# A transformer tower on one core: four max products moved into the expert stage, side stages moved to other tiles, a memset moved to another engine, and two sets of transfers queued elsewhere

## The chip, the cores and the metric

The kernel runs on one core of one Trainium2 chip. The metric is the device time of one execution in microseconds, as a median of repeated runs. Five engines work side by side: TensorE (products), VectorE, ScalarE, GpSimd, and SyncE, which here only issues the transfers.

## The reference

`x` is (16, 64, 128, 64). For each of the 16 items the tower computes, with 1024 tokens of width 64:

```
h = tokens(x)                                    # patches of 16, rfft, @ W.T
h = h + attn0(layernorm(h))                      # 8 heads of 8, bias from a table
h = h + routed_ffn(layernorm(h))                 # in, two layers (one of 16 experts by item part + shared), out
h = h + attn1(layernorm(h))                      # 8 heads of 8
h = h + moe(layernorm(h))                        # gate, top 2 of 8 experts, exact gelu
```

with softmax attention in both layers: `softmax(q @ k.T * scale + bias) @ v`, then a projection.

## The kernel before

**Tiles.** The attentions of all items are one stream of 4096 tiles, 128 for each of the 32 attentions, in `SUPERS` = 4 supertiles of `SUPER` = 32. For a tile `n` TensorE does three things. `scores` (L897): 128 keys by 512 queries in bf16 parts, including three rows with the negated maxima of the queries, written to one of three PSUM banks, the ring `RING`; ScalarE empties it with the exponential (L1101). `nat` (L885), here called the max product: the same kind of product, queries by keys, for a later tile; VectorE reduces it to a row maximum (L1294, `reduce_tile`). It runs `SUPER + LEAD` = 46 tiles ahead of `scores`, over three banks `NAT` of its own. `pv` (L911), the value product: once in four tiles, four heads together, when n % 4 is 1. Each engine's program goes over the tiles in order, and each engine does its instructions in order.

**The maxima's way.** When the last max product of a supertile is reduced, `super_max` (VectorE) and `split_max` (GpSimd, four small steps) make three bf16 parts. The side stage `TN` (`turn`, tiles 23, 55, 87, ...) transposes them on TensorE (L869), VectorE copies them out (L1287), and SyncE writes them into the query rows with four transfers (`max_dma`, L607). `scores` of the next supertile, nine tiles after `TN`, waits for these.

**Pairs and side stages.** `program_phases` makes a serial start, a `first` phase of 128 tiles, 15 pairs of 256 tiles, a `last` phase of 128, and a serial end. Pair `r` runs attention 0 of item r+1 and attention 1 of item r. All other work is cut into named side stages that `side_schedule` puts on tiles of the pair. For each tile TensorE does the side stages first, then its score and max product; ScalarE does the exponential first and then the side stages; VectorE the reduction and then the side stages; GpSimd and SyncE follow the tile order too. The names:

- `LX`: load of an item's x rows, in two halves of 1 MB (L532, two transfers of 512 KB each, SyncE). `TOKA`, `TOKB`, `TOKC`: tokens from the first half, the second half (L750, 8 f32 products), and their transposition (L757).
- `LN1`, `LN2`: layernorm by VectorE and GpSimd in turn; `TR`: transposition of its result (L765). `QK`, `QV`: projections (L772, L727); ScalarE empties QK's two banks, VectorE those of QV. GpSimd then splits q and k into parts (L1400 to L1406), `SCR` writes them to DRAM scratch (L625, L627), and `RL`, the reload, fetches them in 24 transfers into the rows that the products read (L641, L645), 12 for heads 0 to 3 and 12 for heads 4 to 7. `VC` copies v.
- `CT` (two parts), `OTR`, `PROJ`: end of an attention. `H1`, `L0`, `L1`, `WO`: routed feed-forward; `WCL`, `WCA`: loading and summing its weights.
- `GATE`, `RANK`, `MT`, `FW`, `FY0` to `FY8`, `OUT`: mixture of experts. `FW`, the expert stage (L840, L842), runs its eight experts in all four banks, two for each expert in turn: expert e waits for the Gelu of expert e - 2 (L1073). No tile is in work meanwhile.
- `ZK` (pairs 0 and 14): zeroes rows of a key buffer that changes its use.

`SIDE_BANKS` says which stages write into the second side bank. That bank is one of the three ring banks; `score_ring` keeps it from the tiles for `SIDE_TILES` = 4 tiles, so the tiles have two banks in that time.

`middle_of` is the chain from the end of attention 0 to the q, k, v of attention 1, laid out wide over the second half of a pair. `short_middle_of` is the same chain where it has to be done within one half: at the start of pair 0 and in the second half of pair 14.

**SyncE.** `SCR` and `RL` in most phases wait for the score product of their own tile before each transfer is issued. In pairs 0 and 14 they did not: all 24 transfers of the reload stand on one tile (`every=0`) and are issued as soon as the scratch is written. The x rows' second half stands on tile 83 and the max rows on tile 87, both issued in that order.

Of the kernel before, what the change touches and what calls it, by code (L numbers as in the profile page):

```python
# [54 lines left out]
TURN = 23  # L55
SIDE_TILES = 4
# [70 lines left out]
def side_schedule(r, f1, f2, f3, first=False, last=False):  # L127
# [9 lines left out]
    def middle_of(b, n):  # L137

        for dn, name, *more in ((0, "CT"), (5, "OTR"), (8, "PROJ", 0), (13, "LN1", "a"),
# [3 lines left out]
            put(n + dn, name, b, *more)  # L143

    def short_middle_of(b, n):

        for dn, name, *more in ((0, "CT"), (4, "OTR"), (6, "PROJ", 0), (8, "LN1", "a"),
# [4 lines left out]
            put(n + dn, name, b, *more, every=0 if name in ("SCR", "RL") else 2)  # L152
# [25 lines left out]
    if f2:  # L178
        put(78, "TOKA", r + 2)
        put(83, "LX", r + 2, 1)  # L180
        put(97, "TOKB", r + 2)
        put(102, "TOKC", r + 2)
        put(105, "LN1", r + 2, "0")
# [8 lines left out]
    if f3:  # L192
        put(96, "WCL", r + 1)
        put(121, "WCA", r + 1)
        if last:
            put(130, "ZK", 0)
            short_middle_of(r + 1, 135)
        else:
            middle_of(r + 1, 133)
# [123 lines left out]
def super_of(kind, it, q):  # L323
# [12 lines left out]
    return a, b, q % 2, q % SUPERS // 2  # L336

# [10 lines left out]
def tower_kernel(nc, x, w_dft, dft, const, onehot, qk_w, v_w, pw, qk_scale, wi, routed, shared, wo, bo,  # L348
                 table, route, wg, w1, b2, w2, out):
    with ExitStack() as ctx:  # L350
# [165 lines left out]
        def _(eng):  # L516
# [144 lines left out]
            def body(kind, it, n0, side, found):  # L661
# [7 lines left out]
                for n in sorted(side):  # L669
                    for k, stage in enumerate(side[n]):  # L670
                        if stage[0] == "TN":
                            max_dma(kind, it, stage[1], found[n, k])
                        else:
                            side_stage(stage, found[n, k],
                                       n0 + n if kind == "first" or kind == "pair" and 0 < it < B - 2 else 0)
# [6 lines left out]
        def _(eng):  # L682
# [55 lines left out]
            def side_stage(stage, n, tile, slot):  # L738
# [89 lines left out]
                elif name == "FW":  # L828
# [4 lines left out]
                    for e in range(E):  # L833
# [9 lines left out]
                        mm.then_inc(fw_ready, 1)  # L843
                    eng.wait_ge(he_ready, at(E * b + E - 1))
# [72 lines left out]
            def body(kind, it, n0, side, found):  # L917
# [11 lines left out]
                for n in range(n_tiles(kind)):  # L929
                    if kind == "first" and n == LATE:  # L930
                        eng.wait_ge(s_rest, N_SET[s_rest])
                    for k, stage in enumerate(side[n]):
                        if stage[0] == "TN":
                            turn(n0, stage[1], found[n, k])
                        else:
                            side_stage(stage, found[n, k], n0 + n, n)
                    ahead = n + SUPER + LEAD
                    q = ahead // SUPER
# [4 lines left out]
                    if kind != "last" or q < SUPERS:  # L943
                        nat(kind, it, n0, ahead)
# [172 lines left out]
        def _(eng):  # L1117
# [63 lines left out]
            def side_stage(stage, n):  # L1181
                name, b, k, is_last, *more = stage
                if name == "ZK":
                    eng.wait_ge(st_ready, ATTN if b == 1 else ATTN * (2 * B - 2))
                    eng.memset(KA[b][64:K_MAX, :, :], 0.0).then_inc(keys_clear, 1)
                elif name == "TOKC":
# [117 lines left out]
            def body(kind, it, n0, side, found):  # L1304
# [11 lines left out]
                for n in range(n_tiles(kind)):  # L1316
# [5 lines left out]
                    ahead = n + SUPER + LEAD  # L1322
                    q = ahead // SUPER
                    if kind != "last" or q < SUPERS:
                        reduce_tile(n0, ahead)
                        if ahead % SUPER == SUPER - 1:
                            super_max(n0, q)
# [10 lines left out]
        def _(eng):  # L1338
# [31 lines left out]
            def side_stage(stage, n):  # L1370
# [3 lines left out]
                if name == "LN1":  # L1374
# [88 lines left out]
            def body(kind, it, n0, side, found):  # L1463
# [6 lines left out]
                for n in range(n_tiles(kind)):  # L1470
                    if kind == "first" and n == LATE:
                        eng.wait_ge(s_rest, N_SET[s_rest])
                    ahead = n + SUPER + LEAD
                    q = ahead // SUPER
                    if ahead % SUPER == SUPER - 1 and (kind != "last" or q < SUPERS):
                        split_max(n0, q)
# [77 lines left out]
```

## Time and profile before

| | |
|---|---|
| median of 3 runs | 4034.71 us (4033.22 to 4037.4) |
| profiled execution | 4041.78 us, span 4040.0 us |
| TensorE busy | 3811.9 us (94%) |
| VectorE busy | 2886.2 us (71%) |
| ScalarE busy | 2619.9 us (65%) |
| GpSimd busy | 860.0 us (21%) |
| mean granted TensorE clock | 0.98 |

The span is the profiled time between the first and the last instruction. Busy shares are means over all stages. In the timelines, a product's row gives its modelled duration of 0.38 us, while the next may start 0.22 us later; the pace is read from the starts. What stands in brackets is the engine's idle time before the instruction and what ended it.

### The profile page before, as it was taken

What the parts mean: (1) busy time and instruction counts of PE and PEld (TensorE: products, weight loads), DVE (VectorE), ACT (ScalarE), POOL (GpSimd) and SP (SyncE); (2) the same over time, 40 slices, a digit from 0 to 9 for tenths busy, and PEclk for the clock granted to TensorE, in tenths of its full rate; (3) what the DMA queues carried; (4) which work ended last, traced back from release to release, by engine and by line L of the source; (5) the groups of instructions that cost most, each with busy time, mean ns of one, the idle gap of its engine ahead of it and who ended that gap; (6) DMA issues with size and microseconds to landing.
All of it is one profiled execution on the core that took longest, in us unless ns stands there. A gap on an engine that the chain in (4) does not pass through costs nothing.

```text
span 4040.0 us, 62363 instructions
## 1 busy us (share of the span) xinstructions
PE 3811.9 (94%) x21508; PEld 1330.2 (33%) x21508; DVE 2886.2 (71%) x4955; ACT 2619.9 (65%) x4768; POOL 860.0 (21%) x1263
## 2 busy tenths in 40 slices
PE   6988999999999999999999999999999999999896
PEld 3223333333333333333333333333333333333232
DVE  3866767778686777867678676777867677777672
ACT  0555767667676666767667676666767667676564
POOL 4122113122121322213122121312213122121211
PEclk7899999999999999999999999999999999999998
DMA  5203211222012122111222122122111222111100
GB/s 106 40 15 60 43 36 33 46 48 44 22 35 56 33 43 43 37 34 33 46 48 43 27 38 49 32 43 47 38 29 33 50 44 43 31 36 25 28 6 6
DMA packets 119067, 156.36 MB, mean 39 GB/s; under 512 B 24847, under 2 KB 66575, under 8 KB 118717
## 3 DMA queue, kind: packets, MB, share of 16 engines
q1 hardware_dynamic: 118753, 152.38, 19.0%
q8 instruction: 172, 2.82, 0.3%
q14 instruction: 142, 1.16, 0.1%
HBM read 120.01 MB, written 29.36 MB: 37 GB/s over the span
## 4 chain that ended last, share of the span: by engine, by line
PE 81%; ACT 8%; issue 4%; DVE 3%; SPq 2%; DMA 1%; POOL 1%; ACTq 0%; POOLq 0%; DVEq 0%
PE acc L911 23%; PE side_st L897 21%; PE nat L885 19%; PE side_st L854 3%; PE side_st L750 3%; PE side_st L727 2%; ACT prob L1101 2%; PE side_st L840 2%; ACT hidden L1073 2%; PE side_st L807 1%; DVE tile_max L1294 1%; ACT hidden L1019 1%; PE side_st L772 1%; SPq L525 1%; PE side_st L765 1%
## 5 line engine op out<-in xcount | busy, mean ns | idle before, releaser
L1294 DVE TENSOR_REDUCE tile_max<-nat 128x1 f32<-128x512 f32 x4096 | 2585.7, 684 | 1002.6 <-PE nat L885 972.0
L1101 ACT ACTIVATE prob<-side_st 128x512 f32<-128x512 f32 x4096 | 2205.8, 600 | 1271.7 <-PE side_st L897 1236.8
L897 PE MATMUL side_st<-q_rows,k_rows 99*128 99x512 bf16 x4096 | 1562.6, 384 | 45.9 <-ACT prob L1101 28.9
L885 PE MATMUL nat<-k_rows,q_rows 96*128 96x512 bf16 x4096 | 1532.2, 385 | 30.2 <-DVE tile_max L1294 24.0
L911 PE MATMUL acc<-prob,v_padded 128*32 128x512 f32 x8192 | 1096.1, 607 | 14.5 <-ACT prob L1101 13.5
L897 PEld LDWEIGHTS side_st<-q_rows,k_rows 99*128 99x128 bf16 x4096 | 398.6, 98 | 1213.9 <-ACT prob L1101 812.1
L885 PEld LDWEIGHTS nat<-k_rows,q_rows 96*128 96x128 bf16 x4096 | 400.8, 98 | 508.4 <-DVE tile_max L1294 276.1
L1455 POOL TENSOR_SCALAR max_parts<-neg_max 128x16 bf16<-128x16 f32 x128 | 26.5, 207 | 1868.4 <-DVE neg_max L1301 1868.3
L911 PEld LDWEIGHTS acc<-prob,v_padded 128*32 128x32 f32 x8192 | 162.3, 108 | 377.4 <-ACT prob L1101 216.0
L840 PE MATMUL side_st<-ln_rows,w 64*128 64x512 f32 x512 | 139.5, 622 | 28.7 <-ACT hidden L1073 23.2
L1380 POOL TENSOR_SCALAR ln_s<-ln_s 128x8 f32<-128x8 f32 x64 | 13.0, 203 | 676.8 <-DVE ln_s L1202 673.2
L1073 ACT ACTIVATE hidden<-side_st,b 128x1024 f32<-128x1024 f32 x128 | 139.0, 1113 | 18.7 <-PE side_st L842 18.5
L750 PE MATMUL side_st<-x_rows,w_patch 128*128 128x512 f32 x248 | 121.4, 635 | 10.2 <-DMA x_rows<-in_x 10.2
L854 PE MATMUL side_st<-hidden,w 128*64 128x512 f32 x512 | 113.4, 595 | 0.0
L1392 POOL TENSOR_TENSOR ln_s<-ln_s,const 128x8 f32<-128x8 f32 x64 | 105.6, 1650 | 12.1 <-POOL ln_s L1389 12.1
L840 PEld LDWEIGHTS side_st<-ln_rows,w 64*128 64x128 f32 x512 | 41.5, 187 | 101.8 <-ACT hidden L1073 81.5
L750 PEld LDWEIGHTS side_st<-x_rows,w_patch 128*128 128x128 f32 x248 | 50.7, 206 | 66.1 <-issue 51.0
L1406 POOL TENSOR_TENSOR hidden<-hidden 128x1024 bf16<-128x1024 f32 x32 | 68.3, 2133 | 5.9 <-POOL hidden L1404 5.9
L1402 POOL TENSOR_TENSOR hidden<-hidden 128x1024 f32<-128x1024 f32 x32 | 68.2, 2131 | 6.2 <-POOL hidden L1400 6.2
L1394 POOL TENSOR_TENSOR centred<-centred,ln_s 128x512 f32<-128x512 f32 x64 | 66.8, 1043 | 11.4 <-POOL ln_s L1392 11.4
L1385 POOL TENSOR_TENSOR squares<-centred 128x512 f32<-128x512 f32 x64 | 66.6, 1041 | 11.7 <-POOL centred L1383 11.7
L807 PE MATMUL side_st<-hidden,group_weights 128*128 128x256 f32 x256 | 66.0, 379 | 1.4 <-ACTq L1038 1.3
(124 smaller groups left out, 1994.5 us busy)
## 6 DMA issues: line engine op xcount, KB each, us to landing
q_rows<-q_scratch SPq DMA_DIRECT2D x576, 64.0 KB
k_rows<-k_scratch SPq DMA_DIRECT2D x192, 192.0 KB
x_rows<-in_x SPq DMA_DIRECT2D x62, 512.0 KB, 6.3
q_scratch<-hidden SPq DMA_DIRECT2D x32, 384.0 KB
k_scratch<-hidden SPq DMA_DIRECT2D x96, 128.0 KB
group_weights<-in_routed SPq DMA_DIRECT2D x64, 129.0 KB, 2.1
q_rows<-max_rows SPq DMA_DIRECT2D x512, 3.0 KB
out_h<-out_rows SPq DMA_DIRECT2D x16, 256.0 KB, 2.1
```

Source lines behind the costliest of these rows:

```text
L727: mm = eng.matmul(both[par][:, j * cols:j * cols + cols], rows[half, j * P:j * P + P], w[half, :], start=(j == 0), stop=True, skip_group_c ...
L750: mm = eng.matmul(bk[:, :], Wf[:, j, :, :].rearrange("p a o -> p (a o)"), xv[:, :, j, :], start=(j == 0), stop=(j == 3))
L807: mm = eng.matmul(bk[:, c:c + 256], WC[:, g, ll, 0:HID], HE[:, ll, g * 256:g * 256 + 256], start=(g % 2 == 0), stop=True, skip_group_check ...
L840: eng.matmul(both[par][:, :], W1[half, e, :], XT[half, :], start=True, stop=False)
L854: mm = eng.matmul(SIDE[0][half, :], w, m, start=(e < 0), stop=(e == E - 1), skip_group_check=True)
L885: eng.matmul(NAT[use % len(NAT)][:, :], QA[u][0:K_NAT, h, c:c + P], KA[u][0:K_NAT, h, kh * 512:kh * 512 + 512], start=True, stop=True)\
L897: eng.matmul(RING[TILE_BANK[n0 + n]][:, :], KA[u][0:K_ALL, h, t * P:t * P + P], QA[u][0:K_ALL, h, half * 512:half * 512 + 512], start=True ...
L911: mm = eng.matmul(ACC[32 * hh:32 * hh + 32, :], VZ[buffer_of(a, b)][:, t, HEADS * g + hh, :], prob[:, (first_tile + hh) % TILES, :], start ...
L1073: eng.activation(HE[:, e, :], both[:, :], ACT.Gelu, bias=b1[:, e:e + 1]).then_inc(he_ready, 1)
L1101: eng.activation(prob[:, n % TILES, :], RING[TILE_BANK[n0 + n]][:, :], ACT.Exp).then_inc(exp_done, 1)
L1294: eng.tensor_reduce(mx[:, q % 2, j // 8, j % 8 // 2, j % 2:j % 2 + 1], NAT[use % len(NAT)][:, :], AX.X, ALU.max).then_inc(nat_free, 1)
L1392: eng.tensor_tensor(ln_s[:, 4, :], ln_s[:, 3, :], half_pow, ALU.pow).then_inc(ln_p, 1)
```

## The change

- `max_tiles` is new and replaces the fixed `n + SUPER + LEAD` on TensorE, VectorE and GpSimd. On the tile with `FW` the max products run `AHEAD` = 4 tiles further ahead: four of them stand between the products of the second and the third expert. Every third tile after it then has none, until the lead is 46 tiles again (tiles 53, 56, 59 and 62 of the pair).
- Side stages in `middle_of` (which starts at tile 135 and not 133), `short_middle_of` and the token stages of the next item but one stand on other tiles.
- The x rows' second half stands on tile 88, behind the max rows of tile 87; `TOKB` on 99 (97 before), `TOKC` on 103 (102).
- In pairs 0 and 14 the reload's transfers stand on a tile each, and those of its second half 15 tiles further on; and these pairs too wait for the score product of each tile.
- `ZK` goes from VectorE to GpSimd, with the waits that it needs there.

```diff
+AHEAD = 4
 def middle_of(b, n):
-        for dn, name, *more in ((0, "CT"), (5, "OTR"), (8, "PROJ", 0), (13, "LN1", "a"),
-                                (20, "LN2", "a"), (21, "BO"), (29, "TR", "a"), (33, "H1"), (38, "L0"),
-                                (44, "L1"), (49, "WO"), (56, "LN1", "1"), (62, "LN2", "1"),
-                                (71, "TR", "1"), (77, "QK", 1), (80, "QV", 1)):
+                                (20, "LN2", "a"), (21, "BO"), (29, "TR", "a"), (32, "H1"), (37, "L0"),
+                                (43, "L1"), (49, "WO"), (56, "LN1", "1"), (62, "LN2", "1"),
+                                (71, "TR", "1"), (76, "QK", 1), (85, "QV", 1)):
 def short_middle_of(b, n):
-                                (42, "TR", "1"), (44, "QK", 1), (46, "QV", 1), (54, "SCR", 1),
-                                (54, "VC", 1), (58, "RL", 1)):
-            put(n + dn, name, b, *more, every=0 if name in ("SCR", "RL") else 2)
+                                (43, "TR", "1"), (46, "QK", 1), (49, "QV", 1), (55, "SCR", 1),
+                                (55, "VC", 1)):
+            put(n + dn, name, b, *more, every=0 if name == "SCR" else 2)
+        for k, part in enumerate(side_parts([("RL", b, 1)])):
+            at[n + (58 + k if k < 4 * PARTS else 73 + k)].append(part)
 # side_schedule
-        put(83, "LX", r + 2, 1)
-        put(97, "TOKB", r + 2)
-        put(102, "TOKC", r + 2)
-        put(105, "LN1", r + 2, "0")
+        put(88, "LX", r + 2, 1)
+        put(99, "TOKB", r + 2)
+        put(103, "TOKC", r + 2)
+        put(106, "LN1", r + 2, "0")
-            short_middle_of(r + 1, 135)
+            short_middle_of(r + 1, 132)
-            middle_of(r + 1, 133)
+            middle_of(r + 1, 135)
+def max_tiles(side, n):
+    def extra(m):
+        for slot in range(m, max(m - 3 * AHEAD, -1), -1):
+            if any(x[0] == "FW" for x in side.get(slot, ())):
+                return AHEAD - (m - slot) // 3
+        return 0
+    return range(n + SUPER + LEAD + (extra(n - 1) if n else 0), n + SUPER + LEAD + extra(n) + 1)
 # SyncE
-                                       n0 + n if kind == "first" or kind == "pair" and 0 < it < B - 2 else 0)
+                                       n0 + n if kind in ("first", "pair") else 0)
 # TensorE, expert stage: after the mask products of expert e
+                        for where in between if e == 1 else ():
+                            nat(*where)
 # TensorE, for each tile
+                    tiles = max_tiles(side, n)
+                    between = [(kind, it, n0, m) for m in tiles[:-1]]
-                    ahead = n + SUPER + LEAD
-                    q = ahead // SUPER
-                    if kind != "last" or q < SUPERS:
-                        nat(kind, it, n0, ahead)
+                    for m in tiles[len(between):]:
+                        if kind != "last" or m < ATTN:
+                            nat(kind, it, n0, m)
 # VectorE
-                if name == "ZK":
-                    eng.wait_ge(st_ready, ATTN if b == 1 else ATTN * (2 * B - 2))
-                    eng.memset(KA[b][64:K_MAX, :, :], 0.0).then_inc(keys_clear, 1)
 # GpSimd
+                if name == "ZK":
+                    alone(eng.wait_ge(st_ready, ATTN if b == 1 else ATTN * (2 * B - 2)))
+                    alone(eng.wait_ge(wc_ready, n["WCA"]))
+                    eng.memset(KA[b][64:K_MAX, :, :], 0.0).then_inc(keys_clear, 1)
+                    alone(eng.wait_ge(keys_clear, 1 if b == 1 else 2))
```

## Rows read from the trace of the kernel before

**Rows 1.** The page: busy us and share of each engine.
```profile
PE 3811.9 (94%) x21508; PEld 1330.2 (33%) x21508; DVE 2886.2 (71%) x4955; ACT 2619.9 (65%) x4768; POOL 860.0 (21%) x1263
```

**Rows 2.** The page's groups: busy, mean ns, idle before, what ended it.
```profile
L885 PE MATMUL nat<-k_rows,q_rows 96*128 96x512 bf16 x4096 | 1532.2, 385 | 30.2 <-DVE tile_max L1294 24.0
```

**Rows 3.** Timeline, TensorE (start us, us): ordinary stretch; then last phase.
```profile
679.88 0.39 PE L897 MATMUL side_st<-q_rows,k_rows 99*128 99x512 bf16 x1
680.10 0.38 PE L885 MATMUL nat<-k_rows,q_rows 96*128 96x512 bf16 x1
...
682.72 0.39 PE L897 MATMUL side_st<-q_rows,k_rows 99*128 99x512 bf16 x1
...
3966.31 0.39 PE L897 MATMUL side_st<-q_rows,k_rows 99*128 99x512 bf16 x1 [0.26 <-ACT prob L1101]
...
3968.87 0.39 PE L897 MATMUL side_st<-q_rows,k_rows 99*128 99x512 bf16 x1 [0.26 <-ACT prob L1101]
```

**Rows 4.** Timeline of pair 3's expert stage, and its line in the waits view.
```profile
1009.28 0.38 PE L842 MATMUL side_st<-mask_rows,mask_far 64*128 64x512 bf16 x2
...
1011.15 1.13 PE L840 MATMUL side_st<-ln_rows,w 64*128 64x512 f32 x4 [1.49 <-ACT hidden L1073]
...
PE side_st L840 <- ACT hidden L1073: 23.2, 16, 1.5
```

**Rows 5.** Timeline of pair 3, TensorE's waits at tiles 130, 133, 169, 213.
```profile
1098.38 0.39 PE L897 MATMUL side_st<-q_rows,k_rows 99*128 99x512 bf16 x1 [0.43 <-ACT prob L1101]
...
1101.77 0.63 PE L780 MATMUL side_st<-const,acc_sb 128*128 128x128 f32 x4 [0.77 <-DVE v_natural L1210]
...
1134.11 0.39 PE L897 MATMUL side_st<-q_rows,k_rows 99*128 99x512 bf16 x1 [1.23 <-ACT prob L1101]
...
1174.56 1.11 PE L727 MATMUL side_st<-w_v,ln_rows 64*128 64x64 f32 x16 [1.03 <-ACT hidden L1019]
```

**Rows 6.** Timeline of GpSimd at the start, and of pair 0.
```profile
1.73 6.92 POOL L1349 MEMSET q_rows<- 35x8192 bf16 x1
...
222.04 3.47 DVE L1185 MEMSET k_rows<- 32x4096 uint32 x1 [0.91 <-PE side_st L897]
...
226.30 0.61 PE L885 MATMUL nat<-k_rows,q_rows 96*128 96x512 bf16 x1 [3.14 <-DVE tile_max L1294]
...
294.78 0.29 PE L869 MATMUL side_st<-ident_b,max_parts 128*128 128x128 bf16 x1 [3.93 <-POOL max_parts L1461]
...
340.01 0.61 PE L897 MATMUL side_st<-q_rows,k_rows 99*128 99x512 bf16 x1 [8.23 <-DMA q_rows<-max_rows]
```

**Rows 7.** Stretches: length, busy by engine, then granted clock, DMA share, GB/s.
```profile
226.00:233.00 7.00, 6.08 (x19) 1.74 (x19) 4.80 (x10) 1.79 (x3) 0.00 (x0) 0.55 0.01 2
...
3744.00:3749.00 5.00, 2.63 (x19) 1.72 (x23) 4.94 (x7) 1.14 (x4) 0.00 (x0) 1.00 0.01 3
...
3768.00:3772.00 4.00, 4.00 (x16) 0.80 (x14) 1.38 (x2) 1.68 (x3) 1.35 (x2) 0.57 0.01 2
```

**Rows 8.** Timeline of pair 14, TensorE at tile 210.
```profile
3834.49 0.61 PE L885 MATMUL nat<-k_rows,q_rows 96*128 96x512 bf16 x1 [5.29 <-DMA k_rows<-k_scratch]
```

**Rows 9.** Timeline and landing times of the x rows: pair 3, then the start.
```profile
1055.68 1.39 SPq L532 DMA_DIRECT2D x_rows<-in_x  x2
...
1060.55 3.08 SPq L607 DMA_DIRECT2D q_rows<-max_rows  x4
...
1065.43 3.60 PE L750 MATMUL side_st<-x_rows,w_patch 128*128 128x512 f32 x8
...
DMA to landing us min/median/max: 4.8/5.6/6.3
...
67.80 1.34 SPq L532 DMA_DIRECT2D x_rows<-in_x  x2
...
76.57 6.46 PE L750 MATMUL side_st<-x_rows,w_patch 128*128 128x512 f32 x8 [10.19 <-DMA x_rows<-in_x]
...
DMA to landing us min/median/max: 8.0/8.0/8.0
```

More of the change, by code:

```diff
@@ L736, in tok_block, with side_stage @@
                 return mm
-            def side_stage(stage, n, tile, slot):
+            def side_stage(stage, n, tile, slot, between=()):
                 name, b, k, is_last, *more = stage
@@ L935, in body @@
                         else:
-                            side_stage(stage, found[n, k], n0 + n, n)
-                    ahead = n + SUPER + LEAD
-                    q = ahead // SUPER
+                            side_stage(stage, found[n, k], n0 + n, n, between)
                     two_banks = TILE_PREV[n0 + n] == ("tile", n0 + n - 2)
@@ L1182, in side_stage @@
                 name, b, k, is_last, *more = stage
-                if name == "ZK":
-                    eng.wait_ge(st_ready, ATTN if b == 1 else ATTN * (2 * B - 2))
-                    eng.memset(KA[b][64:K_MAX, :, :], 0.0).then_inc(keys_clear, 1)
-                elif name == "TOKC":
+                if name == "TOKC":
                     eng.wait_ge(ho0, at(b))
@@ L1321, in body @@
                         ins.then_inc(s_late, 1)
[L1322 to L1327, printed above, removed]
+                    for m in max_tiles(side, n):
+                        if kind != "last" or m < ATTN:
+                            reduce_tile(n0, m)
+                            if m % SUPER == SUPER - 1:
+                                super_max(n0, m // SUPER)
                     for k, stage in enumerate(side[n]):
@@ L1373, in side_stage @@
                     return
-                if name == "LN1":
+                if name == "ZK":
[3 more added lines that the diff above has]
+                    alone(eng.wait_ge(keys_clear, 1 if b == 1 else 2))
+                elif name == "LN1":
                     src = {"0": h0n, "a": h0c, "1": h1n, "m": h1c}[more[0]]
@@ L1472, in body @@
                         eng.wait_ge(s_rest, N_SET[s_rest])
[L1473 to L1476, printed above, removed]
+                    for m in max_tiles(side, n):
+                        if m % SUPER == SUPER - 1 and (kind != "last" or m < ATTN):
+                            split_max(n0, m // SUPER)
                     for k, stage in enumerate(side[n]):
```

## The prediction

> **What bounds the kernel now.** First the busy shares: TensorE 94% of the span, VectorE 71%, ScalarE 65% [rows 1]. Then the costliest groups: nearly everything is the stream of 4096 tiles, each a score product, a max product (the row shown) and a quarter of a value product [rows 2]. The timeline of an undisturbed stretch gives its pace: a score product starts at 679.88 and the fourth one after it at 682.72, so four tiles take 2.84 us, with 0.22 us from one of the eight products to the next and the other 1.1 us for the value product [rows 3]. Where no max products are left, four tiles take 2.56 us, and then ScalarE's exponentials set the pace (0.26 us of waiting in each group). So TensorE's order binds. A pair of 256 tiles takes some 241 us: 64 x 2.84 = 181.8, the rest is side work in line, and stalls. What the change can win is idle time of TensorE, so the third view is the timeline of TensorE with what ended each wait. I counted the score products in it to place each wait on a tile of its pair.
>
> **The four max products in the expert stage.** The mask products of the second expert start at 1009.28; the third expert starts at 1011.15, after ScalarE's table load and first Gelu [rows 4]. TensorE is idle there for 1.49 us, and the waits view has it 16 times, 23.2 us in all. Four products at 0.22 us are 0.88 us. The fourth needs its bank back: first product 1009.50, its reduction (some 0.4 us later, 0.68 us long) ends near 1010.6, so the fourth runs from 1010.7 to 1010.9, before 1011.15. They are hidden by the Gelu; without it they would cost what they save. Later, four tiles out of twelve have no max product. A group of four loses one at most: 2.62 us, above the 2.56 us at which ScalarE binds. I take 0.8 of 0.88 us. It happens in 15 expert stages (the sixteenth, in the serial end, has nothing to put between): **-12 us** (bounds -4, if ScalarE delays the value products, and -13).
>
> **Stages moved to other tiles, in 14 ordinary second halves.** Pair 3 shows what repeats in nearly every pair, the larger waits as rows [rows 5]: 0.77 us (transposing the sums on tile 133, behind VectorE's emptying of QV), 0.36 us (value product of tile 165), 1.23 us (score product of tile 169: H1 holds one ring bank and ScalarE empties H1 before the exponentials), 0.34 us (max rows, tile 192), 1.03 us (QV waits for QK's banks, three tiles behind it), and 0.58 us (VectorE late at tile 110). That is 4.3 us. The edits answer to each: CT two tiles later; H1 on tile 167, where two exponentials get in ahead of its emptying and a value product covers it; WO now between turn 183 and score 192; QV nine tiles behind QK; token stages one tile later. I keep 3.4 us, as QK on tile 127, the same place in its group as the new H1, still has a 0.43 us wait near it. 14 x 3.4 = **-48 us** (bounds -28 and -60). This work itself is not shortened.
>
> **First pair.** VectorE's memset of the key rows takes 3.47 us and stops TensorE for 3.14 us; the granted clock is 0.55 of full in the 7 us after it, the 1.2 GHz level almost throughout [rows 6, 7]. On GpSimd the memset takes 6.92 us and ends long before GpSimd's next duty, LN1 on tile 12. Gain 6 us: the wait and about 3 us of slow products. The turn of tile 55 waits 3.93 us because GpSimd splits QK's output (QK on tile 48) before the maxima of tile 49; with QK on tile 50 the order turns round. With the slow clock behind it and smaller waits, 8 us. Last, the max rows of tile 87 are issued behind the whole reload and 1 MB of x rows; the score product of tile 96 starts at 340.01 after 8.23 us, and the next four tiles lose 2.5 us to the clock. With the second half of the reload and the x rows behind them, 10.5 us. **-24.5 us** (bounds -15 and -29).
>
> **Last pair.** The memset's 2.96 us and what follows give 4 us. TR of tile 177, now on 175 with one more tile behind LN2, and QV give 3.5 us. The 5.29 us wait for key rows at tile 210 [rows 8] stays mostly: its chain (split, scratch, reload) starts one tile earlier. The reload's second half now runs into the max rows of tile 215: some +2 us against 2 us from fewer transfers in flight. **-7.5 us** (bounds -2 and -14). The sum of gains is 12 + 48 + 24.5 + 7.5 = 92 us.
>
> **What speaks against it: the x rows.** In an ordinary pair they were issued at 1055.68, 3.16 us before score product 87, and TOKB began on tile 97 at 1065.43 without waiting [rows 9]. Now they are queued behind the max rows of tile 87 on SyncE, in 14 pairs (0 to 13). SyncE reaches those at 1060.55 and needs 3.08 us for the four. So the x rows are issued at about 1063.75. Landing: the second transfer starts 0.7 us behind the first (two in 1.39 us) and lands 6.3 us after it, 7.0 us in all. That the number counts to the use is seen near the start: the second of two issued from 67.80 on starts at 68.5, its landing is 8.0, and TensorE, waiting for it, begins at 76.57. So now they land at 1070.7. TOKB on tile 99 could begin at 1065.43 plus two tiles and one value product, about 1067.4. **TensorE waits 3.3 us**, everything behind it in TensorE's queue too, and nothing covers it: side work and tiles share the one stream. What was queued behind the x rows on SyncE (the expert weights for tile 121) is not pressed. The 8.2 us of waiting for max rows was only in the first pair, so this part pays in one pair and costs in fourteen.
>
> Then the clock. The wait of 3.14 us was followed by 0.55 over 7 us and one of 2.44 (last pair, before TR of tile 153) by 0.57 over 4, but the last pair's memset wait of 2.96 by 1.00 [rows 7]. At 1.2 GHz, 4 us lose about 1.7 us of the stream, 7 us about 3.3. I take 1.7 us on average for a wait of 3.3 us: nearly always one short stretch, sometimes none, sometimes a long one. So 5.0 us x 14 = **+70 us** (bounds +42: a landing 0.3 us sooner and no slow clock; and +92: 3.3 + 3.3 each).
>
> The Trainium skill (TensorE: Matmul & The Clock Gate, section "HAM oscillation — how this bites in real kernels") says that a product stream which stops for a DMA again and again pays the clock's fall each time. The rows agree for two waits of three. By the rule each of the 14 would pay its 1.7 us or more, which is the sum above or up to 22 us worse; by the 2.96 us row some pay nothing.
>
> **Sum.** -92 + 70 = -22 us on the profiled execution (4041.78 us, span 4040.0, so 1.8 us lie around it). The median of the runs is 4034.71, 0.17% below; I take the same 22 us from it: 4013 us.
>
> **Rivals.** *(A) The x rows do not stall.* If DMA of 1 MB landed within 3.7 us of its issue, or the issue came earlier, only the gains stay: 4034.7 - 92 = 3943 us. Against it: the second transfer lands after 6.3 to 6.6 us in the pairs I looked at, and the distance from score product 87 to the max rows' issue is 1.70 to 1.73 us in all of them. 7%. *(B) The x rows' wait weighs more than all gains*, the other side: TOKB waits 3.3 us and each is followed by the long slow stretch, 6.6 us x 14 = 92, while the moved stages keep only the lower bound (28 in place of 48). 92 - 20 = 72 gained, 92 lost: 4055 us. It decides from 6.6 us for each TOKB at full gains, or 5.1 at the lower ones. For it: the 3.14 us wait had 7 us of slow clock. Against: the 2.44 us wait had 4, and a dense product stream follows at once. 15%. *(C) The stall without the slow clock:* 14 x 3.3 = 46, so 4034.7 - 92 + 46 = 3989 us. For it the 2.96 us row; 15%. *(D) Gain and loss cancel:* the moved stages give 35 us for 48 and the first pair 20 for 24.5: 92 - 17.5 = 74.5 against 70, so 4030 us, no measurable change. 20%. *My forecast* as summed, 4013 with its own range from 3997 to 4026: 43%.
>
> **How the numbers follow.** A change of 0.2% (8 us) is about what a measurement of this kernel can tell from none. Faster: my forecast, A, C and a little of D, 0.43 + 0.07 + 0.15 + 0.03 = 0.68. Same: D's rest and some of B's near side, 0.19. Slower: B's rest, 0.13. The range takes in my forecast, C and D with most of B: 3984 to 4045 leaves out A and B's far end, about 0.16.
>
> **What the profile afterwards would show.** Between the second and the third expert four max products at 0.22 us with the third expert not later than before. In ordinary pairs none of the waits of 1.23 and 1.03 us. In the first pair no 3.14, 3.93 and 8.23 us waits. And TensorE's wait for the x rows, one of 3.3 us on tile 99 in each of 14 pairs, 46 us in the waits view, with more stretches of lower granted clock. If that line is not there, I am wrong by up to 70 us to the fast side. If instead the new H1 or QV show waits of a us, the 48 is wrong.

## The result, and the profile after

The changed kernel takes 4051.64 us (median of 8 runs, 4043.2 to 4059.24), the kernel before 4034.74 us (8 runs beside it, 4033.22 to 4037.81). The ratio is 1.0037 (1.0027 to 1.0047): 0.4% slower, where 0.5% faster was forecast. Rival B (the wait for the x rows outweighs all gains) is the side on which it came out.

The page of the changed kernel, beside [rows 1] and [rows 2]. The groups have busy us, mean ns, idle time before them and what ended most of it:

```profile
span 4049.8 us, 62481 instructions
...
PE 3829.3 (95%) x21508; PEld 1336.9 (33%) x21508; DVE 2882.6 (71%) x4953; ACT 2618.8 (65%) x4768; POOL 871.6 (22%) x1265
...
L902 PE MATMUL nat<-k_rows,q_rows 96*128 96x512 bf16 x4096 | 1532.2, 384 | 24.4 <-DVE tile_max L1309 21.1
...
L765 PE MATMUL side_st<-x_rows,w_patch 128*128 128x512 f32 x248 | 149.8, 760 | 60.9 <-DMA x_rows<-in_x 60.9
```

The same group of token products on the page of the kernel before:

```profile
L750 PE MATMUL side_st<-x_rows,w_patch 128*128 128x512 f32 x248 | 121.4, 635 | 10.2 <-DMA x_rows<-in_x 10.2
```

TensorE is busier by 17.4 us with the same 21508 instructions. The token products have got 50.7 us more of waiting in front of them, and are themselves 28.4 us longer. The timeline of pair 3 (SyncE, then TensorE), beside [rows 9], shows both:

```profile
1043.38 2.97 SPq L622 DMA_DIRECT2D q_rows<-max_rows  x4
1046.46 1.37 SPq L547 DMA_DIRECT2D x_rows<-in_x  x2
...
1050.01 0.38 PE L902 MATMUL nat<-k_rows,q_rows 96*128 96x512 bf16 x1
1053.85 6.22 PE L765 MATMUL side_st<-x_rows,w_patch 128*128 128x512 f32 x8 [3.46 <-DMA x_rows<-in_x]
1059.90 0.38 PE L914 MATMUL side_st<-q_rows,k_rows 99*128 99x512 bf16 x1
```

And the stretches around it (length, busy time of each engine, granted clock, DMA share, GB/s):

```profile
1047.00:1050.00 3.00, 3.00 (x18) 0.91 (x18) 2.64 (x5) 2.06 (x4) 0.00 (x0) 1.00 0.68 164
...
1053.00:1056.00 3.00, 2.15 (x3) 1.12 (x4) 0.00 (x0) 0.00 (x0) 0.00 (x0) 0.50 0.56 149
1056.00:1059.00 3.00, 3.00 (x4) 1.07 (x4) 0.00 (x0) 0.00 (x0) 0.00 (x0) 0.51 0.00 0
1059.00:1062.00 3.00, 3.00 (x17) 0.94 (x15) 1.46 (x3) 1.67 (x4) 0.00 (x0) 1.00 0.00 0
```

The x rows are issued at 1046.46, behind the max rows; TensorE stands for 3.46 us, and the eight f32 products that follow run for most of their time at the 1.2 GHz level (0.50 and 0.51 in the stretches from 1053 to 1059) and take 6.2 us instead of 3.6. It is so in all 14 pairs: the waits are 3.33 to 3.99 us, 3.63 on average, and over the eight products the granted clock is 0.53 to 0.71, so they run at the 1.2 GHz level for more than half of their time.

The expert stage of pair 3, beside [rows 4], and its group on the page:

```profile
993.13 0.38 PE L857 MATMUL side_st<-mask_rows,mask_far 64*128 64x512 bf16 x2
993.45 0.82 PE L902 MATMUL nat<-k_rows,q_rows 96*128 96x512 bf16 x3
994.62 0.39 PE L902 MATMUL nat<-k_rows,q_rows 96*128 96x512 bf16 x1 [0.35 <-DVE tile_max L1309]
995.01 1.13 PE L855 MATMUL side_st<-ln_rows,w 64*128 64x512 f32 x4
...
L855 PE MATMUL side_st<-ln_rows,w 64*128 64x512 f32 x512 | 139.7, 623 | 5.9 <-ACTq L1080 1.3
```

Four max products stand between the experts, the fourth after a short wait for its bank, and the third expert starts 1.88 us after the second's mask products (1.87 before). The second half of the same pair, beside [rows 5]:

```profile
1096.02 0.63 PE L803 MATMUL side_st<-const,squares 128*128 128x128 f32 x4 [0.77 <-DVEq L1243]
...
1122.49 0.39 PE L914 MATMUL side_st<-q_rows,k_rows 99*128 99x512 bf16 x1 [0.60 <-ACT prob L1119]
...
1129.67 0.39 PE L914 MATMUL side_st<-q_rows,k_rows 99*128 99x512 bf16 x1 [0.74 <-ACT prob L1119]
...
1163.36 0.39 PE L914 MATMUL side_st<-q_rows,k_rows 99*128 99x512 bf16 x1 [0.43 <-ACT prob L1119]
```

The old waits of 0.77, 0.36, 1.23, 0.34 and 1.03 us are gone (3.73 us). In their place stand 0.77 (tile 140), 0.19 (149), 0.60 (170), 0.74 (177), 0.36 (209) and 0.43 (214): 3.09 us.

### The profile page after: what moved, and what is told of

Read it like the earlier page. It is cut to its first block, busy times and chain, and to the rows that moved or that the text cites. A ratio compares the mean times of both kernels' runs of the same rounds, so it can differ in the third digit from the quotient of the medians.

```text
span 4049.8 us, 62481 instructions
## 1 busy us (share of the span) xinstructions
PE 3829.3 (95%) x21508; PEld 1336.9 (33%) x21508; DVE 2882.6 (71%) x4953; ACT 2618.8 (65%) x4768; POOL 871.6 (22%) x1265
## 4 chain that ended last, share of the span: by engine, by line
PE 77%; ACT 7%; DVE 5%; issue 4%; DMA 3%; SPq 1%; POOL 1%; ACTq 0%; DVEq 0%; POOLq 0%
PE acc L928 21%; PE side_st L914 20%; PE nat L902 18%; PE side_st L765 3%; PE side_st L871 3%; DVE tile_max L1309 3%; DMA x_rows<-in_x 2%; ACT prob L1119 2%; PE side_st L855 2%; PE side_st L742 2%; PE side_st L822 2%; ACT hidden L1091 1%; ACT hidden L1037 1%; SPq L622 1%; PE side_st L787 1%
## 5 line engine op out<-in xcount | busy, mean ns | idle before, releaser
L765 PE MATMUL side_st<-x_rows,w_patch 128*128 128x512 f32 x248 | 149.8, 760 | 60.9 <-DMA x_rows<-in_x 60.9
L765 PEld LDWEIGHTS side_st<-x_rows,w_patch 128*128 128x128 f32 x248 | 59.6, 248 | 137.1 <-DMA x_rows<-in_x 68.7
```

Of the source, the lines that this page charges most:

```text
L765: mm = eng.matmul(bk[:, :], Wf[:, j, :, :].rearrange("p a o -> p (a o)"), xv[:, :, j, :], start=(j == 0), stop=(j == 3))
```

## The experiments

Each edit is one against the changed kernel, except where it says otherwise. To see where time goes, I took the starts of the 4096 score products from each trace and averaged the length of stretches of tiles over pairs 1 to 13 (us). A stretch that an edit does not touch mostly agrees within 0.02 us from kernel to kernel. The exceptions, up to 0.16 us, come from single pairs: in the kernel before, the second halves of pairs 5 (low clock behind one wait) and 8 (1.49 us for the max rows at tile 160) are 1.7 us longer than the others, and in mid_h1 that of pair 7 is 1.6. Pairs 0 and 14 vary more: the five kernels x_back, mid_back, mid_qv, mid_h1 and mid_all have the same schedule in the first half of pair 0 and in the whole of pair 14, and still take 129.1 to 131.8 us and 237.9 to 242.3 us there.

```
tiles     before  after  x_back x_only tokb_102 mid_back no_ahead ahead_6 hold_3 mid_qv mid_h1 mid_all
  0- 48    39.79  39.78  39.77  39.79  39.78    39.77    39.78    39.77   40.72  39.77  39.77  39.78
 48- 52    22.72  22.72  22.72  22.72  22.73    22.72    22.72    23.86   22.51  22.72  22.72  22.73
 52- 64     9.19   8.17   8.16   9.19   8.16     8.16     9.19     8.17    8.16   8.18   8.18   8.16
 96-100     6.28  12.41   6.28  12.16   2.85     6.28     6.28     6.28    6.28   6.28   6.28   6.28
100-112    11.46  10.36  10.35  10.35  16.60    10.35    10.35    10.36   10.35  10.36  10.36  10.36
128-144    16.68  16.46  16.46  16.67  16.45    16.68    16.46    16.47   16.02  16.68  16.68  16.68
160-188    28.92  28.89  28.90  28.91  28.89    28.92    28.90    28.90   28.13  28.91  29.37  28.96
188-204    12.63  11.68  11.68  12.63  11.68    12.62    11.68    11.68   11.68  12.62  12.12  12.12
204-228    20.58  20.87  20.87  20.58  20.87    20.46    20.87    20.87   20.83  19.95  20.58  19.96
pair      241.27 244.72 238.58 246.08 242.80   238.97   239.62   239.66  238.10  238.46  239.03  238.00
```

**x_back: the x rows issued on tile 83 again, ahead of the max rows.**

```diff
-        put(88, "LX", r + 2, 1)
+        put(83, "LX", r + 2, 1)
```

> The kernel after the change with one number different: the x rows' second half stands on tile 83 again, ahead of the max rows of tile 87; TOKB stays on tile 99. Theory: TensorE's wait for the x rows (3.33 to 3.99 us in 14 pairs, 50.7 us) and the slow clock behind each are the whole loss. Tiles 96 to 99 of pairs 1 to 13 took 12.41 us after the change and 6.28 before, so each pair gives back 6.1 us: 4051.6 - 86 = 3966 us, and the groups of TOKB fall back to a mean near 600 ns. Rival 1: the max rows then land late at tile 96 in ordinary pairs and part of it comes back as waits there; more than 3980 us. Rival 2: the slow clock is a matter of the whole kernel and stays: about 4000 us.

Measured: 3969.34 us (3965.91 to 3971.73), ratio 0.9833 (0.982 to 0.9847) to the kernel before. The stretch 96 to 100 falls from 12.41 us to 6.28, and nothing else moves by more than 0.02 us in the table. One line of the schedule costs 82 us in the changed kernel (84 when each is taken against the kernel before in its own rounds), and everything else in the change is worth 1.7%. Its page and its stretches around the second half's tokens:

```profile
L765 PE MATMUL side_st<-x_rows,w_patch 128*128 128x512 f32 x248 | 116.8, 615 | 10.1 <-DMA x_rows<-in_x 10.1
```

```profile
1028.00:1035.00 7.00, 7.00 (x43) 1.92 (x42) 6.38 (x12) 5.16 (x10) 0.00 (x0) 1.00 0.36 76
1035.00:1042.00 7.00, 7.00 (x33) 2.95 (x30) 2.94 (x6) 3.04 (x7) 0.00 (x0) 1.00 0.24 59
```

No wait, full clock throughout.

**x_only: the kernel before (so the diff is against it) with the x rows behind the max rows** and the token stages on the new tiles.

```diff
-        put(83, "LX", r + 2, 1)
-        put(97, "TOKB", r + 2)
-        put(102, "TOKC", r + 2)
-        put(105, "LN1", r + 2, "0")
+        put(88, "LX", r + 2, 1)
+        put(99, "TOKB", r + 2)
+        put(103, "TOKC", r + 2)
+        put(106, "LN1", r + 2, "0")
```

> The kernel before with only the x rows' second half on tile 88 and the token stages on 99, 103 and 106. Theory: the same wait with the slow clock, 6.1 us in 14 pairs, less the 1.1 us that tiles 100 to 111 gained after the change, and some 4 us from max rows that no longer stand behind x rows in the first pair: 4035 + 70 - 4 = 4101 us. Rival: the wait comes from something else in the change, and this kernel stays within 8 us of 4035.

Measured: 4096.98 us (4085.3 to 4099.93), ratio 1.014 (1.0124 to 1.0156). The waits are again 14, 3.68 us on average. The cost stands by itself and does not need the rest of the change.

Pair 0 of this run shows one thing more. All 24 transfers of the reload still stand on one tile here, and yet the wait of 8.23 us for the max rows ([rows 6]) is gone; the last row is the score product of tile 96:

```profile
326.90 3.05 SPq L607 DMA_DIRECT2D q_rows<-max_rows  x4
330.07 1.36 SPq L532 DMA_DIRECT2D x_rows<-in_x  x2
331.35 0.38 PE L897 MATMUL side_st<-q_rows,k_rows 99*128 99x512 bf16 x1
```

So that wait needed both, the reload on one tile and the x rows ahead of the max rows, and the new order takes it away by itself.

**tokb_102: the x rows stay behind the max rows, their use three tiles later.**

```diff
-        put(99, "TOKB", r + 2)
-        put(103, "TOKC", r + 2)
-        put(106, "LN1", r + 2, "0")
-        put(114, "LN2", r + 2, "0")
-        put(123, "TR", r + 2, "0")
+        put(102, "TOKB", r + 2)
+        put(106, "TOKC", r + 2)
+        put(109, "LN1", r + 2, "0")
+        put(117, "LN2", r + 2, "0")
+        put(124, "TR", r + 2, "0")
```

> The kernel after the change, x rows still behind the max rows, but TOKB on tile 102, TOKC 106, LN1 109, LN2 117, TR 124: three tiles and a value product more ahead of TOKB, 2.4 us. Theory: the wait shrinks from 3.65 to about 1.2 us, and as the 1.49 us waits in the expert stage left the clock alone, so does this: 6.1 - 1.2 = 4.9 us less in 14 pairs, 3983 us, no low clock in ordinary pairs. Rival: any wait for a DMA in each pair costs the clock too, some 2.5 us more each: about 4018 us.

Measured: 4027.2 us (4022.34 to 4034.97), ratio 0.9977 (0.9968 to 0.9986). The waits view, us in total, times, longest:

```profile
PE side_st L914 <- ACT prob L1119: 36.4, 81, 0.7
PE acc L928 <- ACT prob L1119: 29.0, 60, 1.1
PE side_st L780 <- POOL centred L1413: 28.9, 20, 9.4
PE side_st L765 <- DMA x_rows<-in_x: 28.8, 15, 10.5
```

Thirteen of the waits for x rows are now 1.0 to 1.6 us, and there the eight products take 3.7 us at full clock; the one of 2.23 us (pair 11) is followed by 1.2 GHz and 5.4 us:

```profile
2993.50:2998.90 5.40, 5.39 (x9) 2.23 (x10) 0.00 (x0) 0.00 (x0) 0.00 (x0) 0.68 0.01 3
...
1051.70:1055.40 3.70, 3.67 (x9) 1.63 (x10) 0.00 (x0) 0.00 (x0) 0.00 (x0) 1.00 0.19 55
```

So the clock's part goes when the wait is short, as the theory had it and against the rival, whose 4018 us is nearer all the same; but new places wait, as in pair 3: a value product at tile 105 for ScalarE (1.13 us), a max product at 113 (0.58), the transposition at 124 for GpSimd (0.52). Tiles 96 to 128 take 34.4 us here and 30.2 in x_back, and 14 times this difference is 59 us, all that parts the two kernels. That is why 4027 and not 3983 came out: stages that are moved bring their own waits.

**mid_back: x_back, with `middle_of` at its old place and offsets.**

```diff
-                                (20, "LN2", "a"), (21, "BO"), (29, "TR", "a"), (32, "H1"), (37, "L0"),
-                                (43, "L1"), (49, "WO"), (56, "LN1", "1"), (62, "LN2", "1"),
-                                (71, "TR", "1"), (76, "QK", 1), (85, "QV", 1)):
+                                (20, "LN2", "a"), (21, "BO"), (29, "TR", "a"), (33, "H1"), (38, "L0"),
+                                (44, "L1"), (49, "WO"), (56, "LN1", "1"), (62, "LN2", "1"),
+                                (71, "TR", "1"), (77, "QK", 1), (80, "QV", 1)):
...
-            middle_of(r + 1, 135)
+            middle_of(r + 1, 133)
```

> As x_back, and the chain from attention 0 to attention 1 in ordinary pairs on its old tiles (start 133, H1 33, L0 38, L1 44, QK 77, QV 80). Theory of the failed step: the moved stages gave 0.66 us in a pair and not 3.4, as the waits only went elsewhere: 9 us slower than x_back. Rival: they are worth 3.4 us, hidden in the comparison by the slow clock: 48 us slower than x_back. Second rival: nothing, equal within 3 us.

Measured: 3972.01 us (3970.01 to 3973.62), 2.7 us above x_back, with ranges that overlap; by number this is the second rival (equal within 3 us) and not the 9 us of the theory. The table has 0.39 us in a pair, which would be 5.5 us in 14. Re-timing the whole second half, where 3.73 of the 4.3 us of waits stood, was worth 0.4 us in a pair. This is the failed step, seen alone.

**mid_qv and mid_h1: one re-timing at a time.** The first is mid_back with only QK and QV on the new tiles, the second with only H1, L0 and L1 on theirs and WO on 184.

```diff
-                                (71, "TR", "1"), (77, "QK", 1), (80, "QV", 1)):
+                                (71, "TR", "1"), (78, "QK", 1), (87, "QV", 1)):
```

```diff
-                                (20, "LN2", "a"), (21, "BO"), (29, "TR", "a"), (33, "H1"), (38, "L0"),
-                                (44, "L1"), (49, "WO"), (56, "LN1", "1"), (62, "LN2", "1"),
+                                (20, "LN2", "a"), (21, "BO"), (29, "TR", "a"), (34, "H1"), (39, "L0"),
+                                (45, "L1"), (51, "WO"), (56, "LN1", "1"), (62, "LN2", "1"),
```

> As mid_back (237.0 to 239 us a pair, mean 238.97), with QK on tile 211 and QV on tile 220 alone moved. Theory: the 1.03 us wait of QV goes and waits near tile 214 come: 0.3 to 0.5 us less a pair. Rival by the prediction: 1.0 us less a pair, as only 0.43 us can come back and 1.03 and some slow emptying go.

> As mid_back, with H1 on tile 167, L0 on 172, L1 on 178 and WO on 184 alone moved. Theory: the 1.23 us wait at tile 169 splits into one at 170 and one at 177 and tiles 160 to 187 stay at 28.9 us; only the 0.34 us for the max rows at tile 192 goes: 0.4 us less a pair. Rival by the prediction: 1.3 us less a pair.

Measured, one run each: 3965.84 us with a pair of 238.46, and 3975.02 us with a pair of 239.03 (mid_back 238.97). QV takes away the 1.03 us wait and keeps 0.51 us of it. H1 takes away 1.23 us and gets 0.60 and 0.74 in its place, from the timeline of mid_h1:

```profile
1098.51 0.39 PE L914 MATMUL side_st<-q_rows,k_rows 99*128 99x512 bf16 x1 [0.60 <-ACT prob L1119]
...
1105.70 0.39 PE L914 MATMUL side_st<-q_rows,k_rows 99*128 99x512 bf16 x1 [0.74 <-ACT prob L1119]
```

Its stretch 160 to 188 is 0.45 us longer than in mid_back; the 0.50 us that it wins in 188 to 204 is WO's, as mid_all below, which differs from mid_qv in WO alone, wins the same there. So the forecast of 0.4 us less a pair for mid_h1 did not hold: the pair is 0.06 us longer (0.04 shorter in the median pair), which is WO's gain and a loss of 0.4 to 0.5 us with H1, L0 and L1.

**hold_3: x_back, with the ring bank kept from the tiles for three tiles in place of four.**

```diff
-SIDE_TILES = 4
+SIDE_TILES = 3
```

> As x_back with SIDE_TILES = 3: a ring bank that a side stage used is kept from the tiles for three tiles, not four. Theory: the waits of 0.60 and 0.74 us at tiles 170 and 177 come from running on two banks while ScalarE empties; with one tile less of it they shrink, but a tile then waits for the emptying itself: between 1 us less and 1 us more a pair, tiles 160 to 187 not at 28.9 us. Rival: the waits are ScalarE's or VectorE's order alone and the pair keeps 238.6 us within 0.2.

Measured: 3958.05 us (one run), pair 238.10. The 0.60 us wait at tile 170 is gone and the one at 177 is 0.33, so 0.77 us less in 160 to 188: the exponential that is waited for there is a matter of the held bank. A new wait of 0.64 us for VectorE at tile 9 takes back more than that (0 to 48: +0.95), but 48 to 52 and 128 to 144 are shorter too (0.21 and 0.44), so the pair is 0.48 us shorter than x_back's.

**no_ahead and ahead_6: x_back with none and with six max products in the expert stage.**

```diff
-AHEAD = 4
+AHEAD = 0      # no_ahead
+AHEAD = 6      # ahead_6
```

> As x_back with AHEAD = 0: no max product in the expert stage, the lead stays at 46 tiles. Theory: the four products are hidden by the first Gelu, and tiles 52 to 63 of each pair go from 8.16 back to 9.19 us: 15 x 1.0 = 15 us slower than x_back (3969), 3984 us. Rival: the stage was no shorter for it and the 1.0 us comes from the stages of tiles 53 to 56; then no more than 3 us slower.

> x_back with six max products in place of four behind the second expert's opening ones. Theory: four products of some 0.25 us just fill the hole of about 1 us there; the two more find it full or wait for bank buffers that are not yet reduced, and push the third expert back. Stretch 52 to 64 goes from 8.16 us to 8.6 to 9.4 us, the whole to 3976 to 3988 us. Rival: room is left in the hole, six are as good as four or better: stretch at 8.16 us or less, 3966 to 3970 us.

Measured: 3982.94 us (3980.14 to 3984.85) with none, 13.6 above x_back, and 3985.14 us with six (one run). The page of no_ahead has the wait for the Gelu back:

```profile
L855 PE MATMUL side_st<-ln_rows,w 64*128 64x512 f32 x512 | 140.2, 625 | 28.3 <-ACT hidden L1091 22.8
```

With six, the timeline shows that from the fourth on each one waits for a reduction, and the third expert starts at 979.74, 3.01 us behind the second's mask products in place of 1.88:

```profile
976.73 0.38 PE L857 MATMUL side_st<-mask_rows,mask_far 64*128 64x512 bf16 x2
977.05 0.82 PE L902 MATMUL nat<-k_rows,q_rows 96*128 96x512 bf16 x3
978.22 0.39 PE L902 MATMUL nat<-k_rows,q_rows 96*128 96x512 bf16 x1 [0.35 <-DVE tile_max L1309]
978.82 0.39 PE L902 MATMUL nat<-k_rows,q_rows 96*128 96x512 bf16 x1 [0.21 <-DVE tile_max L1309]
979.42 0.39 PE L902 MATMUL nat<-k_rows,q_rows 96*128 96x512 bf16 x1 [0.21 <-DVE tile_max L1309]
979.74 1.13 PE L855 MATMUL side_st<-ln_rows,w 64*128 64x512 f32 x4
```

The loss stands in 48 to 52 (+1.14), not in 52 to 64 where I had looked for it.

**zk_back: x_back with the memset on VectorE.**

```diff
 # VectorE; out of GpSimd in the same way
+                if name == "ZK":
+                    eng.wait_ge(st_ready, ATTN if b == 1 else ATTN * (2 * B - 2))
+                    eng.memset(KA[b][64:K_MAX, :, :], 0.0).then_inc(keys_clear, 1)
```

> x_back with the clearing of the keys' upper rows (ZK) put back from GpSimd to VectorE; all else as x_back, so only the first pair and the pair before the end can change. Theory: where VectorE clears, its reductions stand 8.2 us behind in the first pair and TensorE waits for bank buffers: the first pair takes 5.7 us more than x_back's 239.54 us, the pair before the end about 4.3 us more than 239.26 us, the whole about 10 us more than x_back, 3979 us. Rival: the clearing was hidden and the shorter stretch at the start of the first pair came from the re-timed stages alone: within 2 us of x_back's 3969.3 us.

Measured: 3977.32 us (one run). Pair 0 takes 244.70 us (x_back 239.54), pair 14 246.83 (239.26). The 3.15 us wait at pair 0 is back:

```profile
220.32 0.41 PE L902 MATMUL nat<-k_rows,q_rows 96*128 96x512 bf16 x1 [3.15 <-DVE tile_max L1312]
```

In pair 14 waits of 2.34 and 2.41 us follow each other with the clock at 0.50, so 7.6 us are lost there, more than the 4.3 expected. In the kernel before, the memset's wait of 2.96 us in that pair left the clock at 1.00 ([rows 7]), so the 7.6 us are not what the memset had cost there.

**reload_back: x_back with the short middle's 24 transfers on one tile and no waiting for tiles in pairs 0 and 14.**

```diff
-            at[n + (58 + k if k < 4 * PARTS else 73 + k)].append(part)
+            at[n + 58].append(part)
...
-                                       n0 + n if kind in ("first", "pair") else 0)
+                                       n0 + n if kind == "first" or kind == "pair" and 0 < it < B - 2 else 0)
```

> x_back with all parts of the short middle's reload issued at one tile again, and the maximum rows of the first pair and of the pair before the end issued without waiting for their tile, as in the kernel before. Theory: the wait for maximum rows near tile 96 of the first pair comes back (8.4 us of the first pair's gain was there), and a smaller one near tile 210 of the pair before the end (2 to 3 us): 3978 to 3981 us. Rival: the two halves of this edit are redundant with the re-timed stages, nothing comes back: within 2 us of 3969.3 us.

Measured: 3976.51 us (one run), pair 0 247.52 us (+8.0; tiles 64 to 100 alone +8.7), pair 14 242.38 (+3.1). SyncE and TensorE in pair 0:

```profile
302.72 1.36 SPq L547 DMA_DIRECT2D x_rows<-in_x  x2
307.59 3.13 SPq L622 DMA_DIRECT2D q_rows<-max_rows  x4
...
319.15 0.61 PE L914 MATMUL side_st<-q_rows,k_rows 99*128 99x512 bf16 x1 [6.96 <-DMA q_rows<-max_rows]
```

In pair 14 it is not the max rows that come back, as I had expected, but the key rows (5.13 us here, 3.16 in x_back, 2.76 to 4.76 in the other kernels with a tile for each transfer, 5.29 and 5.92 in the two others without). The 3.1 us of the pair are within what pair 14 varies by itself, as mid_h1, with the spread reload, has 242.29 us too:

```profile
3770.37 0.61 PE L902 MATMUL nat<-k_rows,q_rows 96*128 96x512 bf16 x1 [5.13 <-DMA k_rows<-k_scratch]
```

**mid_all: x_back with the re-timings that paid (QK, QV, WO) and the rest of the second half at the old tiles.**

```diff
-                                (20, "LN2", "a"), (21, "BO"), (29, "TR", "a"), (32, "H1"), (37, "L0"),
-                                (43, "L1"), (49, "WO"), (56, "LN1", "1"), (62, "LN2", "1"),
-                                (71, "TR", "1"), (76, "QK", 1), (85, "QV", 1)):
+                                (20, "LN2", "a"), (21, "BO"), (29, "TR", "a"), (33, "H1"), (38, "L0"),
+                                (44, "L1"), (51, "WO"), (56, "LN1", "1"), (62, "LN2", "1"),
+                                (71, "TR", "1"), (78, "QK", 1), (87, "QV", 1)):
...
-            middle_of(r + 1, 135)
+            middle_of(r + 1, 133)
```

> x_back with only those re-timings of the ordinary second halves kept that paid in the single trials: the value and key stages of the second half at tiles 211 and 220, WO at 184, the rest where the kernel before had it. Theory: mid_qv's pair of 238.46 us less up to 0.34 us for the wait at tile 192: 238.1 to 238.5 us, the whole 3961 to 3967 us, under x_back's 3969.3 us and far under both kernels. Rival: each wait taken away comes back at the next stage, as the others did: 3968 us or more.

Measured: 3961.25 us (3956.09 to 3962.92), ratio 0.9807 (0.9794 to 0.9821): faster than both kernels. 14 x 0.58 us (238.58 less 238.00) is 8.1 us, and the medians of x_back and mid_all differ by 8.1; that they agree to the tenth is chance. WO alone (mid_all against mid_qv) is worth 0.46 us in a pair.

## Why the prediction was wrong, point by point

Forecast were 92 us of gains and 70 of loss; the runs show about 68 of gain (x_back against its own kernel before: 4036.93 - 3969.34) and 82 to 86 of loss (4051.64 - 3969.34, and 14 times the 6.13 us of the table).

- **The moved stages, 48 us (3.4 us for each of 14 second halves): the step that failed.** Tiles 128 to 256 became 0.66 us shorter in a pair (the sum of that half's stretches, before against x_back) and tiles 96 to 128 0.96 (the token stages: 1.11 in 100 to 112, less 0.14 behind it), 1.6 us in all, 14 x 1.6 = 23 us. In the median pair the second half is only 0.38 us shorter, as mid_back has it too (0.39); the rest of the 0.66 is what held up pairs 5 and 8 of the kernel before, so 14 x 1.35 = 19 us is the safer figure. Both are below even my lower bound of 28. I had added up the waits that would vanish, and they did vanish; what I had not done is to follow the next instruction of each stage at its new tile. Taken singly, QV gave 0.51 us in a pair and WO 0.46, H1 with L0 and L1 took 0.4 to 0.5, and all of them with CT two tiles later came to 0.39. The 1.23 us wait returned as 0.60 and 0.74, the 0.77 us one as 0.77 at OTR. I had written that waits at the new H1 or QV would show the 48 wrong; they stand at tiles 170, 177 and 214. What ends the new 0.77 us wait (VectorE, L1243) was read, not tried by itself.
- **The x rows: right mechanism, undersized.** The wait was forecast at 3.3 us and measured 3.63; of the chain, the time from issue to landing holds (7.0 forecast; 1046.46 to 1053.85 is 7.4). The clock's part was forecast at 1.7 us and measured 2.5: the stretch 96 to 100 is 6.13 us longer, less 3.63. I had averaged over rows where the clock sometimes stayed up; here it fell in 14 of 14. 14 x 6.13 = 86 for 70. The Trainium skill (TensorE: Matmul & The Clock Gate, section "HAM oscillation — how this bites in real kernels") tells of a loop that stops for a DMA of some 3 to 5 us in each pass, and pays the clock's fall in each. For the waits of 3.3 to 4.2 us the traces agree, 28 times of 28 in the changed kernel and x_only; the 13 waits of 1.0 to 1.6 us in tokb_102, shorter than those of the section, paid nothing.
- **The four max products, 12 us: right.** 13.6 us by no_ahead, 1.03 us in each stretch 52 to 64, and of the 23.2 us of [rows 4] the page of the changed kernel has 5.9 us left in front of that group for all causes. Six products showed the bound that I had argued with: the reductions are the limit behind the third.
- **The first pair, 24.5 us: right.** Pair 0 went from 264.25 us to 239.54 in x_back, 24.7; 1.0 of it is the expert stage and 1.3 the moved stages behind tile 100, so 22.4 us are the first pair's own. The memset is worth 5.2 us there by zk_back (6 forecast); tiles 16 to 64, where the 3.93 us wait stood, are 6.9 us shorter, 5.8 without the expert stage (8 forecast); tiles 64 to 100 are 10.8 shorter (10.5 forecast). For the last I had taken the reload and the x rows behind the max rows together. Each suffices by itself: x_back has the gain with the x rows in front, x_only has no wait for max rows with the reload on one tile, and only with neither (reload_back) do 8.0 us come back.
- **The last pair, 7.5 us: 9.8 measured** (249.10 to 239.26), 1.0 of it the expert stage. The parts came out otherwise than forecast, and that the sum is near has some luck in it. By stretches, the kernel before against x_back: tiles 128 to 144, where the memset's wait stood, are 4.3 us shorter (4 forecast); tiles 144 to 160 are 4.0 longer and 160 to 188 5.2 shorter, so the re-timed stages there gave 1.2 on balance (3.5 forecast for TR and QV); tiles 210 to 228 are 3.2 shorter, where I had put nothing, as the 5.29 us wait of [rows 8] was to stay. It is 3.16 in x_back. Between the five kernels with the same schedule there, 128 to 144 and 160 to 188 agree within 0.1 us, but 144 to 160 varies by 0.9 and 210 to 228 by 3.6 (16.8 to 20.5), so the last part may be chance in part.
- **The net** came to +17 us by medians and not -22: 25 to 29 us from the moved stages, some 12 to 16 from the x rows; what the other three terms missed nearly cancels. Rival B named both (6.6 us for each x wait, moved stages at 28) and gave 4055; the runs have 6.1 and 19 to 23.

## What to carry to other kernels

A wait that is moved away from one instruction is no gain until the instructions behind it, at their new places, have been followed to where they end; in a schedule this dense a re-timing kept half of the wait that it removed (QV) or less than nothing (H1), so each is tried alone and only those that pay are kept (mid_all). A fix for a stall that happens once (here 8 us in the first pair) should be tied to the pair where it happens, because its price is paid in every pair: here it could be had without the reordering that cost 82 us. And the price of a stall in a dense product stream is the stall and the slow products behind it, so it pays first to make it short, even where it can't be removed.

## What the runs showed of the hardware that was not expected

For the waits on the x rows, the clock went with the wait's length: in the changed kernel and x_only, 28 waits of 3.3 to 4.2 us were each followed by the 1.2 GHz level over some or all of the eight token products (which then took 4.9 to 6.6 us up to the next tile, and 3.4 at full clock in x_back); in tokb_102, 13 waits of 1.0 to 1.6 us never were, and the single one of 2.23 us was (0.68 over the next 5.4 us). The same kind of wait therefore cost between 1.5 and 3.2 us more than its own length, with nothing in the program to tell which.

Other waits in the same traces do not fit one order of lengths. The wait of 2.96 us in [rows 7] was followed by full clock. One of the fourteen waits of 1.03 us for QV in the kernel before (pair 5) was followed by 0.85 and 0.69, which the others were not:

```profile
1657.29 1.11 PE L727 MATMUL side_st<-w_v,ln_rows 64*128 64x64 f32 x16 [1.03 <-ACT hidden L1019]
...
1657.00:1660.00 3.00, 2.71 (x26) 1.27 (x26) 1.56 (x4) 1.72 (x4) 2.38 (x2) 0.85 0.02 5
1660.00:1664.00 4.00, 4.00 (x21) 1.20 (x17) 2.22 (x6) 2.13 (x4) 3.62 (x3) 0.69 0.00 0
```

And short waits close to each other went with a low clock too, in pair 0 of the changed kernel, and at the same stages in pairs 0 and 14 of the kernels made from it:

```profile
239.81 0.29 PE L886 MATMUL side_st<-ident_b,max_parts 128*128 128x128 bf16 x1 [1.42 <-POOL max_parts L1480]
242.13 2.08 PE L813 MATMUL side_st<-ln_rows,w_in 64*128 64x512 f32 x4 [1.18 <-DVE max_rows L1302]
...
238.00:240.00 2.00, 0.58 (x4) 0.19 (x3) 0.69 (x1) 1.08 (x2) 1.11 (x5) 0.94 0.00 0
240.00:243.00 3.00, 1.82 (x5) 0.58 (x5) 0.88 (x2) 0.60 (x1) 0.00 (x0) 0.50 0.01 3
```
